# A masked graph layer on one core: the correction for unused gather slots computed on GpSimd instead of ScalarE

## The reference

```python
# layer 0
h = relu(layernorm(x));  mask = adj > 0
xj = h @ W1a
e[j,k] = relu(xj[j] + (h[j] - h[k]) @ W1b + b1)        # H = 192 values for each edge
hm[j]  = sum_k mask[j,k] * e[j,k];  deg[j] = sum_k mask[j,k]
x = x + hm @ W2 + deg * b2
# layer 1
h = relu(layernorm(x))
x = x + (adj @ h) @ W.T
```

## Time and profile before

| | |
|---|---|
| median of 3 runs | 945.11 us (942.63 to 945.84) |
| the profiled execution | 940.0 us, of which the span is 938.2 us |
| TensorE | busy 95% of the span |
| VectorE | busy 94% |
| ScalarE | busy 89% |
| GpSimd | busy 62% |
| granted TensorE clock | 0.989 of full speed (mean) |
| DMA engines | 95% busy in the first fortieth of the span, then next to nothing |

### The profile page before, as it was taken

One profiled execution on the slowest core, in us unless ns is written; L12 is line 12 of the kernel. 1 busy time (PEld: TensorE's weight loads), 2 busy tenths in 40 slices (PEclk: granted clock), 3 DMA queues, 4 the chain that ended last, 5 costly groups with the idle time before them and its releaser, 6 DMA issues.

```text
span 938.2 us, 28102 instructions
## 1 busy us (share of the span) xinstructions
PE 889.5 (95%) x9138; PEld 818.6 (87%) x9139; DVE 885.7 (94%) x3032; ACT 832.2 (89%) x1856; POOL 582.1 (62%) x1420
## 2 busy tenths in 40 slices
PE   3879999999999999999999999999999999999996
PEld 1459999999999999999999999999999999999995
DVE  6999999999999999999999999999999999999993
ACT  3978999999999999999999999999999999899993
POOL 0856666666666665666666665666666666656664
PEclk9799999999999999999999999999999999999998
DMA  9500000000000000000000000000000000000000
GB/s 340 223 1 2 7 8 2 8 8 7 8 7 8 7 2 8 7 7 8 8 7 2 8 8 6 9 8 6 2 7 8 7 8 9 7 5 4 8 7 15
DMA packets 8114, 19.18 MB, mean 20 GB/s; under 512 B 1312, under 2 KB 5920, under 8 KB 6944
## 3 DMA queue, kind: packets, MB, share of 16 engines
q1 hardware_dynamic: 7056, 16.98, 4.8%
q10 hardware_dynamic: 912, 0.39, 0.2%
HBM read 13.17 MB, written 4.19 MB: 19 GB/s over the span
## 4 chain that ended last, share of the span: by engine, by line
PE 64%; DVE 25%; ACT 4%; issue 4%; POOL 1%; DMA 1%; DVEq 0%; SPq 0%; ACTq 0%; POOLq 0%
PE ring L353 31%; DVE acc L745 13%; PE post L438 8%; PE ring L379 5%; DVE onehot_space L729 5%; PE post L439 4%; ACT ring L502 3%; PE prep L409 3%; PE post L442 2%; PE prep L419 2%; PE prep L416 2%; PE prep L415 2%; DVE onehot_row L781 2%; DVE owner L775 1%; DMA x_all<-x_nbf_dram 1%
## 5 line engine op out<-in xcount | busy, mean ns | idle before, releaser
L502 ACT COPY ring<-P 128x768 f32<-128x768 f32 x512 | 405.2, 814 | 44.0 <-DVE acc L745 35.1
L353 PE MATMUL ring<-PQ,onehot_space 128*128 128x192 f16 x4096 | 401.0, 246 | 18.1 <-ACT ring L502 14.6
L353 PEld LDWEIGHTS ring<-PQ,onehot_space 128*128 128x128 f16 x4096 | 341.1, 99 | 29.8 <-DVE onehot_space L729 17.1
L745 DVE SCALAR_TENSOR_TENSOR acc<-ring,acc 128x768 f32<-128x768 f32 x384 | 362.2, 943 | 0.7 <-PE ring L353 0.7
L828 POOL TENSOR_TENSOR relu_row<-relu_row 128x192 f32<-128x192 f32 x256 | 154.4, 603 | 255.5 <-ACT relu_row L538 245.5
L729 DVE TENSOR_SCALAR onehot_space<-mask_all 128x256 f16<-128x256 f16 x1024 | 230.4, 266 | 0.0
L438 PE MATMUL post<-consts,acc 128*128 128x128 f32 x1024 | 154.4, 273 | 1.5 <-POOL relu_row L828 1.5
L745 DVE SCALAR_TENSOR_TENSOR acc<-ring,start 128x768 f32<-128x768 f32 x128 | 121.7, 951 | 28.3 <-PE ring L353 28.1
L438 PEld LDWEIGHTS post<-consts,acc 128*128 128x128 f32 x1024 | 114.2, 141 | 1.6 <-issue 1.6
L439 PE MATMUL post<-ownerT,relu_row 128*128 128x128 f32 x512 | 99.0, 275 | 0.0
L379 PE MATMUL ring<-PQ,owner 128*128 128x384 f16 (+1 forms) x512 | 93.9, 306 | 0.0
(11 more groups left out here) (129 smaller groups left out, 1609.1 us busy)
## 6 DMA issues: line engine op xcount, KB each, us to landing
adj_all<-adj_kbj_dram SPq DMA_DIRECT2D x8, 1024.0 KB, 17.9
x_all<-x_nbf_dram SPq DMA_DIRECT2D x8, 512.0 KB, 18.6
out_dram<-x_all SPq DMA_DIRECT2D x32, 128.0 KB, 1.7
consts<-consts_dram SPq DMA_DIRECT2D x1, 192.0 KB, 2.6
onehot_space<-w1a_dram ACTq DMA_DIRECT2D x2, 48.0 KB, 4.2
onehot_space<-w1b_dram ACTq DMA_DIRECT2D x2, 48.0 KB, 6.9
onehot_space<-b_dram ACTq DMA_DIRECT2D x1, 96.0 KB, 9.8
w2a<-w_dram ACTq DMA_DIRECT2D x1, 32.0 KB, 11.3
```

The source lines that it names most:

```text
L353: last = nc.tensor.matmul(to, hot(s), parts[:, part, H:2 * H], start=False, stop=(part == 1), skip_group_check=True)
L502: return nc.scalar.copy(slots[to], src.unsqueeze(1).unsqueeze(1).broadcast_to([N, BANKS, PER_BANK, H]))
L745: return nc.vector.scalar_tensor_tensor(sums, slots[to], 0.0, so_far, ALU.max, ALU.subtract if first else ALU.add)
```

## The change

`start` is computed by GpSimd from the f32 copy of P in SBUF, where ScalarE computed it from PSUM. In the unrolled form it is one instruction (multiply by `spare`, maximum with 0), in the looped form two. It stands between L847 and L851 in GpSimd's list, behind a wait for `p_ready` and for the first `consume` of the current graph (`summed`), which frees `start`. VectorE's two waits for `start_ready` that protected its reads of `prep` become waits for `p_ready`. For graph 0, GpSimd computes it after its prologue.

```diff
-            def start_sums(b):
-                nc.scalar.activation(start[:, 0, :], pq_ps[:, 0:H], ACT.Relu, scale=spare[:, bass.ds(b, 1)]).then_inc(start_ready, 1)
...
                         nc.scalar.copy(P[:, (u + 1) % 2, :], pq_ps[:, 0:H]).then_inc(p_ready, 1)
-                        if main:
-                            start_sums(b + 1)
...
             act.wait_ge(tables_ready, 1)
-            act.wait_ge(pq_ready, 1)
-            start_sums(0)
             act.wait_ge(ring_ready, 1)
...
                     if i == 3 and main and exists(b + 1):
-                        dve.wait_ge(start_ready, b + 2)
+                        dve.wait_ge(p_ready, b + 2)
                         second_part(b + 1, u + 1)
...
                         if exists(b + 1):
-                            dve.wait_ge(start_ready, b + 2)
+                            dve.wait_ge(p_ready, b + 2)
                         nc.vector.tensor_tensor(x_all[:, b - 2, :], x_all[:, b - 2, :], out1_ps, ALU.add).then_inc(x1_ready, 1)
...
         def _(pool):
+            def start_sums(b, u):
+                if isinstance(b, int):
+                    nc.gpsimd.tensor_scalar(start[:, 0, :], P[:, u % 2, :], spare[:, b:b + 1], 0.0, ALU.mult, ALU.max).then_inc(start_ready, 1)
+                else:
+                    nc.gpsimd.tensor_tensor(start[:, 0, :], P[:, u % 2, :], spare[:, bass.ds(b, 1)].broadcast_to([N, H]),
+                                            ALU.mult).then_inc(product_ready, 1)
+                    wait_apart(pool, product_ready, b - BODY)
+                    nc.gpsimd.tensor_scalar(start[:, 0, :], start[:, 0, :], 0.0, None, ALU.max).then_inc(start_ready, 1)
...
                     pool.wait_ge(p_ready, b + 2)
+                    if exists(b):
+                        pool.wait_ge(summed, b * REGULAR + 1)
+                        start_sums(b + 1, u + 1)
                     nc.gpsimd.tensor_tensor(PQ[:, (u + 1) % 2, 1, 0:H], P[:, (u + 1) % 2, :], PQ[:, (u + 1) % 2, 0, 0:H],
                                             ALU.subtract).then_inc(p_part_ready, 1)
...
             pool.wait_ge(tables_ready, 1)
+            pool.wait_ge(p_ready, 1)
+            start_sums(0, 0)
             graphs(nc.gpsimd, step, some)
```

More of the change, by code:

```diff
@@ L204, in gnn_kernel @@
         start_ready = sem("start_ready")
+        product_ready = sem("product_ready")
         onehot_ready = sem("onehot_ready")
```

## The result

The changed kernel takes 961.03 us (median of 4 runs, 955.85 to 964.37), the kernel before 944.41 us beside it (942.63 to 945.84): the ratio is 1.0172, 95% interval 1.0123 to 1.0222. It is slower by 16.6 us, where 12.7 us were forecast. The profiled execution, the fastest of the four, takes 955.85 us with a span of 953.8 us, 15.6 us more than before's 938.2 (busy shares of before: the earlier trace rows).

What follows compares the result with a forecast made beforehand. Even steps were taken as bound by TensorE, odd ones by VectorE. Over 62 pairs, 0.185 us each gave 11.5 us, plus 1.2 us for the first step: 945.1 + 12.7 = 957.8 us, range 938 to 970.

Steps and rivals of the forecast that it cites:

- the prediction's own signs of being wrong: New instruction taking 0.4 us or less, VectorE's triple of one-hots undisturbed, or ScalarE's wait for GpSimd not growing.
- ScalarE's gain is 0: ScalarE loses L506, 0.46 us a step, but its wait for GpSimd's shift grows from 0.20 to about 0.66 us.
- GpSimd's instruction, 0.55 us with bounds 0.40 and 0.65: Assumed duration of the new 128x192 `start` instruction on GpSimd, taken from L851's row of the same width.
- From above: Upper bound for `start` on GpSimd: one-input rows of 1 and 64 columns carried on to 192, about 0.65 us.
- Even step, triple +0.23: Even step: L851 moves 0.55 us later, so VectorE's three one-hots of the extra rows end at 508.42 instead of 508.19.
- Head of the odd step, +0.12: Odd step's start: `relu_row` and GpSimd's pair L828 come 0.2 us later, so the second `consume` starts 0.12 us later.
- Odd step, -0.10 or +0.23, average +0.065: Odd step's triple on VectorE: ends 0.10 us earlier in one kind of odd step, 0.23 us later in the other.
- First step, +1.2: Graph 0: the first `consume` waits for GpSimd's prologue and 0.55 us of `start`, beginning near 58.05; 1.2 us, once.
- Taking both as equally frequent: The two kinds of odd step, triple -0.10 or +0.23 us, were given equal weight, making +0.065 us.
- The walk itself: Tracing the 0.55 us instruction through an even and an odd step's VectorE and GpSimd rows: 0.185 us a pair, 11.5 us.
- the delay carries on: Rival: GpSimd as a whole starts 0.23 us later in odd steps, both kinds of triples lose 0.23 more; 972 us, chance 0.10.
- The rule on the shared port: VectorE and GpSimd share a port pair as an exclusive lock, kept for a whole instruction; by it L851 delays the triple.

## Why the prediction was right, and where it was not

The time came out inside the range and 0.3% from the forecast, 961.0 against 957.8; the sign and the engine that pays are right. The working is right in part only, errors in it offset each other, and the nearness is luck: the same two kernels differ by 16.6 us here and by 9.1 us on another chip (948.75 against 939.61), where 12.7 were forecast. One of the prediction's own signs of being wrong came true: the triple is undisturbed in even steps.

- **ScalarE's gain is 0**: right as to its wait, which grew from 0.22 to 0.53 us a step (0.66 forecast). Its busy time fell by 41 us and not by 59, 0.32 us a step: the row of L506 begins at 506.44 while L552 before it runs until 506.58, so that not all of its 0.46 us came free. In the version without `start` a gain of 0.6% came in another way, by the odd steps' form.
- **VectorE's and the new `summed` wait cost 0**: right, nobody waits for `start` beyond the first step.
- **GpSimd's instruction, 0.55 us with bounds 0.40 and 0.65**: wrong, 0.945. "From above" was carried on from a form with one operation and a constant, and was no upper bound. GpSimd's busy time rose by 116 us, not 70.
- **Even step, triple +0.23**: wrong, 0 (0.38 us as before). With 0.94 us the split comes behind the triple's start, not ahead of it.
- **Head of the odd step, +0.12**: wrong, 0, since the even step passed on no delay.
- **Odd step, -0.10 or +0.23, average +0.065**: wrong in size, right in place. It is 0 in a short step and +0.26 in a long one, 0.19 a pair with the five more long ones: 11.1 us in 57 pairs, where the forecast's three terms together gave 0.185 a pair, 11.5 us in 62. That agreement is luck.
- **First step, +1.2**: it is 2.3. GpSimd's `start` began at 58.85 and took 0.93 us, and it began 0.67 us behind the prologue's end, which the forecast had not counted:

```profile
58.85 0.93 POOL L818 TENSOR_SCALAR start<-P,spare 128x192 f32<-128x192 f32 x1 [0.67 <-issue]
...
59.82 0.96 DVE L738 SCALAR_TENSOR_TENSOR acc<-ring,start 128x768 f32<-128x768 f32 x1 [2.17 <-POOL start L818]
```

- **"Taking both as equally frequent"** was the sentence that hid the real cause. I saw two kinds of odd steps and averaged over them instead of asking what made them.
- **The walk itself** was tested with the instruction that it assumed: the triple took 0.63 us in even steps, the first `consume` of the odd step was followed by the second 1.91 us later, and the kernel took 967.55 us, 27.7 us or 3.1% more. The rival "the delay carries on" had 26.9 us more, the forecast 12.7; at the duration that was assumed, that rival would have been the right case. The rule that a held triple ends 0.30 us behind GpSimd's instruction was short by 0.1 us: the split ends at 501.81, the triple at 502.21.
- **The rule on the shared port** ("SBUF — State Buffer", section "SBUF: two separate sides", of the Trainium skill) holds for the two-input instructions: 0.63 us a triple. For GpSimd's one-input `start` it does not: across the triple from end to end, it cost 0.04 us. The measurement decides.

No run here shows why a one-input instruction of GpSimd lets VectorE through; and what shifts add and one-hot by those few ns from step to step and from chip to chip stays open.

## What to carry to other kernels

When a tight schedule shows two forms of the same step in one trace, find out what decides between them before costing anything, and judge a change by the number and length of each form; two medians alone may show little more than how often each form came up. Moving work to an engine with room can cost through which neighbour it pushes against which instruction of a full engine: one swap in GpSimd's order, with what it moved elsewhere, took the whole cost of the change back (0.9992). Price a GpSimd instruction by a row of the same form (inputs, operations, multiplier), not only of the same size.

## What the runs showed of the hardware that was not expected

- GpSimd's two-input instruction of 128x192 takes 0.51 to 0.59 us and the one-input one with two operations 0.94 us: the one with less to read is the slower.
- The two-input one stops VectorE's f16 one-hots while it runs, the one-input one hardly (0.63 against 0.42 us for the triple, 0.38 undisturbed).
- Which of a GpSimd add and a VectorE one-hot is held turned over within a few ns: in the odd steps of before the one-hot was held where the add started 37 to 46 ns ahead of it, the add was held where it started 30 to 32 ns ahead, and in between, at 33 to 36 ns, it was either.
- A 0.14 us instruction more on VectorE in every other step, 64 in all, made the kernel 1% faster.
